# Four edits and a new instruction order in a fused decoder kernel: squared key lengths from the diagonal of the key product, weights packed on chip, row-grouped mask, padded spreading

## The chip, the cores and the metric

The kernel runs on one core of a Trainium2 chip. The metric is device time of one launch, in microseconds (us). A core has five engines that run their own instruction streams and meet only at semaphores: TensorE (PE: matrix products, with its weight loads shown as PEld), VectorE (DVE), ScalarE (ACT), GpSimd (POOL) and SyncE (SP), which here only issues DMAs.

## The reference, cut to what matters

32 sequences of 128 tokens and 256 features pass through a gated-delta-rule block with a top-2 mixture of experts (steps named `a_...` and `b_...` in the kernel), a cross attention to a context of 128 tokens, and a routed column layer (steps `c_...`). The lines that the change touches:

```python
mixed = jax.nn.silu(causal_dwconv(mixed, conv_w))          # a_conv, a_mix
q, k, v = jnp.split(mixed, [KEY_DIM, 2 * KEY_DIM], axis=-1)
q = q * jax.lax.rsqrt(jnp.sum(q * q, -1, keepdims=True) + EPS)
k = k * jax.lax.rsqrt(jnp.sum(k * k, -1, keepdims=True) + EPS)
...
# gated delta rule: S = S*exp(g); delta = (v - k S) * beta; S = S + k delta; o = q S
```

The cross attention adds a mask to its scores before the softmax over 16 heads of 16 features, and its projections use the weights Wq and Wk. The column layer picks the best of 16 columns for each token (a one-hot row) and multiplies the 1024 hidden values of the token by that row, spread from 16 to 1024 values.

## The kernel before, in words

One sequence is one item. All weights stay in SBUF. The work on an item is cut into about 75 named steps for PE and as many for the other engines; every engine runs a loop of 35 trips, and in a trip it runs the steps in the order of its list in `ORDER` (line 111). A step with `@1` works on an item one trip older than its letter says: `a` steps work on the item of this trip, `b` on the one before, `c` on the one two trips back, and the suffix gives the lag where it differs. So in a steady trip three or four items are in work, and an engine never leaves the order of its list: an instruction that waits holds up all that stands behind it. After the first trip each engine waits once, in `before_b`, for the second group of weights (semaphore `w_b`).

The steps that the change and the prediction speak of, in their order on PE:

- `a_ss`, `a_st` (lines 483 to 494): the lengths of q and k. ACT squares `mixed` into `sqk` (`a_sq`, L839, 1024 columns), PE sums it over the partitions with a 32-column block of ones (L487, four column groups of 256 columns), ACT copies the sum (L843), PE transposes it in two pieces (L493), DVE adds epsilon into `sse` (L1018). POOL's `a_sc` takes the power -0.5 of it and builds `krb`, `ckk`, `irk`, `eyec` and `pairc`.
- `a_kk` (L518): the product of the keys with themselves, four heads of 128x128 in bank A1. DVE's `a_lower` multiplies it by the decay (L1030), and `a_init` starts the triangular inverse from it (L1049 to L1060).
- `a_dec0`, `a_dec1` (L510, L511): exponents of the decay. `a_dec1` writes bank A3, in which the lengths were, and so waits for `sse_ok` first; ACT takes their exponential (L854).
- `c_wT`, `c_spread` (L748, L755): the one-hot is transposed to 16 partitions, copied by ACT (L970), and spread by eight bf16 products with a contraction of 16.
- `c_pj0`, `c_pj1` (L761): the column layer's second product; DVE's `c_gc0`, `c_gc1` (L1233) feed it. `c_weight` (L1218 to L1227) is the softmax weight, which `c_sum3` (L1239) uses.
- `b_x2T` (L623): waits for `x2`, which DVE writes in `b_x2` (L1119) behind `c_sum3`, `b_hid` (L1096) and `c_y3` (L1107 to L1103).
- `a_la..`, `a_lb..` (L535, L545): the levels of the inverse, 32x32 blocks that alternate with DVE (L1068, L1073, L1075).
- `b_dn`, then DVE's `b_ys` (L1142) and `b_y1` (L1107), `b_y1T` (L663), `b_q` (L670), with the copies of q on ACT (L919) and of k on DVE (`b_k`, L1153).
- `c_s` (L681, L685): the mask goes into four banks by four bf16 products of 512 columns with a contraction of 128 (identity times the filled mask), and the scores are added to it in four row groups of 32. Then DVE's `c_max` (L1161), ACT's `c_exp` (L926), PE's `c_pT` (L692).

At the start SP issues every load one after the other (lines 412 to 424). The weights Wq and Wk come from a DRAM layout with 16 used and 16 empty columns alternating, and 16 DMAs (`dense_qk`) gather the used ones.

## Time and profile before

| | us |
|---|---|
| median of 3 runs | 2304.79 (2304.69 to 2305.6) |
| the profiled execution | 2305.36, with a span of 2303.6 from first to last instruction |
| PE busy | 2130.6 (92%) |
| DVE busy | 1657.9 (72%) |
| ACT busy | 1374.1 (60%) |
| POOL busy | 778.8 (34%) |

The page gives for each engine the time in which it ran something. PE's figure is the largest by far, and the chain that ended last runs through PE for 77% of the span and through DVE for 14%. Busy is the time in which a matrix product was under way, and matmuls overlap in the pipeline, so two starts are closer than a duration. The page's strip of the span shows the same picture in every slice but the first two and the last ones: the kernel repeats one trip.

### The profile page before, as it was taken

How to read it: one execution, taken by the hardware profiler on the slowest of the kernel's cores; microseconds unless marked ns; L12 is line 12 of the kernel's file. 1: busy time of each engine (PE TensorE's matmuls, PEld its weight loads, DVE VectorE, ACT ScalarE, POOL GpSimd, SP SyncE). 2: the span in 40 equal slices, each digit the busy share in tenths (PEclk: the TensorE clock that was granted, in tenths of full speed). 3: DMA queues.
4: the chain of work that ended last, by engine and by line, in shares of the span. 5: the costliest groups of instructions: out<-in, count | busy, mean ns of one | idle time of the engine just before them, and what ended most of it. 6: DMA issues, size and time to landing. Idle time of an engine off the chain costs nothing.

```text
span 2303.6 us, 81126 instructions
## 1 busy us (share of the span) xinstructions
PE 2130.6 (92%) x33068; PEld 1805.7 (78%) x33130; DVE 1657.9 (72%) x5290; ACT 1374.1 (60%) x4262; POOL 778.8 (34%) x1835
## 2 busy tenths in 40 slices
PE   4799999999999999999999999999999999999976
...
DMA packets 33954, 30.12 MB, mean 13 GB/s; under 512 B 17680, under 2 KB 31008, under 8 KB 32816
## 3 DMA queue, kind: packets, MB, share of 16 engines
...
q14 instruction: 107, 0.88, 0.1%
...
## 4 chain that ended last, share of the span: by engine, by line
PE 77%; DVE 14%; ACT 4%; issue 3%; SPq 2%; POOL 1%; DVEq 0%; DMA 0%; POOLq 0%
PE bank_b L641 11%; PE bank_a L463 10%; PE bank_b L738 5%; PE bank_a L473 4%; PE bank_b L761 4%; PE bank_b L649 4%; PE bank_b L602 4%; DVE y1p L1142 3%; PE bank_a L579 3%; PE bank_a L535 3%; PE bank_a L511 3%; PE bank_b L692 3%; ACT prob L926 2%; PE bank_a L586 2%; PE bank_a L545 2%
## 5 line engine op out<-in xcount | busy, mean ns | idle before, releaser
L1013 DVE SCALAR_TENSOR_TENSOR acc<-ypad,convw,acc 128x128 f32<-128x128 f32 x1536 | 429.0, 343 | 112.4 <-ACT acc L815 112.1
L463 PE MATMUL bank_a<-xnT,wqkvz 128*128 128x128 f32 x2048 | 250.6, 279 | 2.0 <-DVE u L1089 2.0
L463 PEld LDWEIGHTS bank_a<-xnT,wqkvz 128*128 128x128 f32 x2048 | 241.4, 194 | 6.2 <-DVE u L1089 4.3
L926 ACT ACTIVATE prob<-bank_b,nmax 128x128 f32<-128x128 f32 x512 | 182.2, 381 | 39.4 <-DVE nmax L1163 38.6
L1378 POOL TENSOR_TENSOR ostat<-ostat 128x4 f32<-128x4 f32 x64 | 20.4, 320 | 504.3 <-ACT gseg L880 502.2
L1424 POOL TENSOR_SCALAR lnv<-mv 128x1 f32<-128x1 f32 x128 | 26.1, 204 | 362.5 <-DVE mv L1103 357.2
L815 ACT ACTIVATE acc<-bank_a,convw 128x128 f32<-128x128 f32 x512 | 148.0, 395 | 0.0
L535 PE MATMUL bank_a<-zblk,kkT 32*32 32x32 f32 x8192 | 119.5, 195 | 22.3 <-DVE zblk L1073 15.6
L906 ACT ACTIVATE prob<-bank_b 128x512 f32<-128x512 f32 x64 | 38.2, 597 | 167.4 <-PE bank_b L641 167.4
L535 PEld LDWEIGHTS bank_a<-zblk,kkT 32*32 32x32 f32 x8192 | 93.7, 107 | 55.8 <-issue 44.5
L545 PE MATMUL bank_a<-ablk,xblk 32*32 32x32 f32 x8192 | 120.0, 195 | 18.6 <-DMA bk<-in_bk_dram 15.1
L1161 DVE TENSOR_REDUCE smax<-bank_b 128x4 f32<-128x512 f32 x128 | 87.7, 685 | 67.8 <-PE bank_b L685 67.8
L545 PEld LDWEIGHTS bank_a<-ablk,xblk 32*32 32x32 f32 x8192 | 96.5, 107 | 49.4 <-issue 44.5
L641 PE MATMUL bank_b<-x2T,wg 128*128 128x128 f32 x1024 | 131.8, 282 | 0.0
L738 PE MATMUL bank_b<-y2T,wc 128*128 128x128 f32 x1024 | 131.2, 283 | 0.0
L641 PE MATMUL bank_b<-x2T,wu 128*128 128x128 f32 x1024 | 128.4, 279 | 0.0
L692 PE MATMUL bank_b<-const,prob 128*128 128x128 f32 x512 | 80.7, 281 | 47.2 <-ACT prob L926 47.2
L649 PE MATMUL bank_b<-wd,prob 128*128 128x256 f32 x512 | 124.1, 385 | 0.0
L738 PEld LDWEIGHTS bank_b<-y2T,wc 128*128 128x128 f32 x1024 | 123.5, 198 | 0.0
L761 PE MATMUL bank_b<-wp,prob 128*128 128x256 f32 x512 | 121.1, 380 | 1.1 <-DVE prob L1233 1.1
L1142 DVE SCALAR_TENSOR_TENSOR y1p<-bank_b,route,y1p 128x256 f32<-128x256 f32 x224 | 107.1, 478 | 20.8 <-DVE y1p L1142 0.5
L641 PEld LDWEIGHTS bank_b<-x2T,wg 128*128 128x128 f32 x1024 | 120.5, 193 | 1.3
...
## 6 DMA issues: line engine op xcount, KB each, us to landing
...
```

The lines of the kernel that those rows point to most:

```text
L463: last = mm(A[bank][:, b * P:(b + 1) * P], wqkvz[:, c, o:o + P], xnT[:, c, :], start=(c == 0), stop=(c == KC - 1))
L535: last = mm(A_LEVEL[half][r, BLK * h:BLK * (h + 1)], kkT[r, h, r], zblk[r, h, :], start=True, stop=True)
L545: last = mm(A_LEVEL[half][r, BLK * h:BLK * (h + 1)], xblk[r, h, :], ablk[r, h, :], start=True, stop=True)
L641: last = mm(Bk[bank][:, b * P:(b + 1) * P], w[:, c, o:o + P], x2T[:, c, :], start=(c == 0), stop=(c == KC - 1))
L649: mm(Bk[DOWN[e]][:, D * (b % 2):D * (b % 2) + D], act_[:, e, :], wd[:, e, :], start=True, stop=True)\
L692: last = tr(Bk[b][:, j * P:(j + 1) * P], prob[:, b, j, :], ident)
L738: last = mm(Bk[2 + half][:, b * P:(b + 1) * P], wc[:, c, o:o + P], y2T[:, c, :], start=(c == 0), stop=(c == KC - 1))
L761: last = mm(Bk[2][:, 0:D], gcw[:, b, :], wp[:, b, :], start=(b == 0), stop=(b == 7))
L815: fn(acc[:, c, :], A[bank][:, b * P:(b + 1) * P], ACT.Copy, scale=convw[:, c, TAPS - 1:TAPS])\
L926: last = fn(prob[:, j, b, :], Bk[j][:, b * P:(b + 1) * P], ACT.Exp, scale=HD ** -0.5, bias=nmax[:, 4 * j + b:4 * j + b + 1], accum_out=esu ...
L1013: stt(acc[:, c, :], ypad[:, c, k:k + P], convw[:, c, k:k + 1], acc[:, c, :], ALU.mult, ALU.add).then_inc(conv.sem, 1)
L1142: stt(y1p[:, :], Bk[DOWN[e]][:, D * (b % 2):D * (b % 2) + D], route[:, e:e + 1], y1p[:, :] if e else xh[:, :], ALU.mult, ALU.add).then_inc ...
```

## The change

1. **Key lengths from the diagonal.** `a_sq`, `a_ss`, `a_st` handle q alone: half the columns, one transpose. A new DVE step `a_kd` waits for the key product and reads the diagonal of each of the four heads with an instruction that multiplies by the identity and sums. `sse_ok` now counts five, one from `a_ss` and four from `a_kd`.
2. **Weights packed on chip.** Wq and Wk are loaded whole by two DMAs into the space of `probT`, and POOL copies the used columns in eight instructions in `before_b`.
3. **Mask in row groups.** Each bank's mask product has a contraction of 32 on its own row group.
4. **Padded spreading.** The one-hot and the spreading matrix have 128 rows, zero beyond 16; POOL clears them once.
5. **New order** of all four lists. Where the steps above stand before and after is in the lists below.

```diff
-    pe="b_v@2 b_x2T@2 a_lb01@1 a_la10@1 b_router@2 b_gu0@2 b_gu1@2 a_la11@1 a_lb10@1 b_gu2@2 a_la20@1 "
-       "a_lb11@1 b_gu3@2 b_dn0@2 a_lb20@1 a_la21@1 b_dn1@2 a_lb21@1 a_vT0@1 a_la30@1 b_k@2 a_la31@1 a_lb30@1 "
-       "a_lb31@1 b_y1T@2 a_pa@1 b_q@2 a_pb@1 c_s a_mt@1 c_pT0 a_vT1@1 a_xT a_sz0@1 c_pT1 a_ba a_qkv0 c_pT2 "
-       "a_o0@1 a_sz1@1 c_pT3 a_qkv1 a_o1@1 c_pv c_R a_z0 a_z1 c_xo a_qkv2 a_qkv3 c_y2T a_dec0 c_h a_ss c_lg "
-       "c_c0 a_st c_c1 c_wT a_kk c_spread a_dec1 c_pj0 b_oT0 b_oT1 c_pj1 b_w0 b_w1 a_la00 b_cT a_qk a_la01 "
-       "a_lb00".split(),
-    act="b_sum@2 b_cT@2 b_x2T@2 b_sg0@2 b_rl@2 b_sg1@2 b_rt@2 a_mix2@1 a_mix3@1 a_sum b_y1T@2 a_zf@1 b_q@2 "
-       "a_zo@1 c_exp0 a_mt@1 c_exp1 a_xT c_exp2 a_sz0@1 c_exp3 a_ba a_qkv0 a_o0@1 a_sz1@1 c_pT0 c_pT1 a_qkv1 "
-       "a_o1@1 c_R a_ln a_z0 a_mix0 a_z1 a_seg a_mix1 a_sq c_y2T c_h a_qkv2 a_st c_lt a_qkv3 c_c0 c_te c_wT "
-       "c_c1 a_dec0 a_dec1 b_oT0 b_oT1".split(),
-    dve="a_lb31@1 a_pa@1 b_k@2 a_u0@1 c_y4@3 c_max0 c_max1 a_xn c_max2 a_low@1 a_u1@1 c_max3 c_pT0 a_conv00 "
-       "a_conv01 c_pT1 a_conv02 c_rec a_core0@1 a_conv10 c_ao a_conv11 a_core1@1 c_sum2 a_conv12 c_y2 c_lb "
-       "c_route a_conv20 a_ss c_gc0 c_weight c_gc1 a_lower a_init c_sum3 b_hid a_la00 c_y3 b_x2 a_la01 "
-       "a_lb00 a_conv21 b_v a_conv22 a_lb01 a_conv30 a_la10 a_conv31 a_la11 a_lb10 b_act0 b_top a_conv32 "
-       "a_la20 a_lb11 a_score b_act1 b_ys0 a_la21 a_lb20 b_ys1 a_lb21 a_la30 a_la31 b_y1 a_lb30".split(),
-    pool="c_y2b@3 a_rq@1 c_ln2@3 b_xh@2 b_rs@2 b_rd@2 b_rt@2 c_ln3@3 a_xr@1 b_ln0@2 b_y1b@2 a_x a_osc0@1 a_ga "
-       "a_osc1@1 a_g c_ln1 c_rx b_mask c_sig a_sc".split(),
+    pe="a_la10@1 b_router@2 b_gu0@2 b_gu1@2 a_la11@1 a_lb10@1 b_gu2@2 a_lb11@1 a_la20@1 b_gu3@2 b_dn0@2 "
+       "a_la21@1 a_lb20@1 b_dn1@2 a_la30@1 a_lb21@1 b_k@2 a_vT0@1 a_la31@1 a_lb30@1 a_lb31@1 b_y1T@2 a_pa@1 "
+       "b_q@2 a_pb@1 c_s a_vT1@1 a_mt@1 c_pT0 a_xT a_sz0@1 c_pT1 a_sz1@1 a_ba a_qkv0 a_o0@1 a_qkv1 c_pT2 "
+       "c_pT3 a_o1@1 c_pv c_R a_z0 a_z1 c_xo a_qkv2 a_qkv3 c_y2T a_dec0 c_h c_c0 c_lg a_ss c_c1 a_st a_kk "
+       "c_wT c_spread a_dec1 c_pj0 b_oT0 b_oT1 c_pj1 b_w0 b_w1 a_la00 b_cT a_la01 a_lb00 a_qk b_v b_x2T "
+       "a_lb01".split(),
+    act="b_oT0@2 a_mix2@1 b_oT1@2 b_sum@2 b_cT@2 b_x2T@2 b_rl@2 b_sg0@2 a_sum b_sg1@2 b_rt@2 a_mix3@1 b_y1T@2 "
+       "a_zf@1 b_q@2 a_zo@1 c_exp0 a_mt@1 c_exp1 a_xT c_exp2 a_sz0@1 a_sz1@1 c_exp3 a_ba a_qkv0 c_pT0 a_o0@1 "
+       "c_pT1 a_qkv1 a_o1@1 a_ln c_R a_z0 a_mix0 a_seg a_z1 a_qkv2 c_y2T a_mix1 a_sq c_h a_qkv3 c_lt a_st "
+       "c_c0 c_c1 c_wT c_te a_dec0 a_dec1".split(),
+    dve="c_max0 a_xn c_max1 a_low@1 a_u1@1 c_max2 c_max3 a_conv00 c_pT0 c_pT1 c_rec a_conv01 a_conv02 "
+       "a_core0@1 a_conv10 c_ao a_core1@1 c_sum2 a_conv11 c_y2 a_conv12 a_conv20 a_conv21 a_conv22 c_lb "
+       "a_conv30 c_route a_ss a_kd c_gc0 c_gc1 a_lower c_weight a_init c_sum3 b_hid a_la00 c_y3 b_x2 a_la01 "
+       "a_lb00 b_v a_score b_top a_lb01 a_conv31 a_la10 a_lb10 b_act0 a_la11 a_la20 a_conv32 a_lb11 b_act1 "
+       "b_ys0 a_lb20 a_la21 b_ys1 a_lb21 a_la30 c_y4 a_la31 b_y1 a_lb30 a_lb31 a_u0 a_pa b_k".split(),
+    pool="b_xh@2 b_rs@2 a_xr@1 b_mask@2 c_ln3@3 a_rq@1 a_x b_rd@2 b_rt@2 b_ln0@2 b_y1b@2 a_ga a_osc0@1 "
+       "a_osc1@1 a_g c_ln1 c_rx c_sig a_sc c_y2b c_ln2".split(),
...
+        ssT = scoreT[:, 0, :]
...
+        raw = probT[:, :, :, :].rearrange("p a b f -> p (a b f)").rearrange("p (w k f) -> p w k f", w=2, k=KC)
+        raw_qk = [(raw[:, i, :, :], w_d) for i, w_d in enumerate((wq_d, wk_d))]
...
+            def a_kd(n):
+                dve.wait_ge(*kk_ps(n))
+                for h in range(HK):
+                    nc.vector.tensor_tensor_reduce(out=diag_junk[:, h, :], in0=A[1][:, h * P:(h + 1) * P], in1=ident, scale=1.0,
+                                                   scalar=EPS_RMS, op0=ALU.mult, op1=ALU.add, accum_out=sse[:, HK + h:HK + h + 1])\
+                        .then_inc(sse_ok.sem, 1)
...
-                mm(quad(Bk[j]), ident_bf[:, :], fill_bf[:, :].unsqueeze(1).to_broadcast([P, 4, P]), start=True, stop=False)
+                mm(quad(Bk[j]), row0_bf[r, :], fill_bf[r, :].unsqueeze(1).to_broadcast([32, 4, P]), start=True, stop=False)
...
-                tr(Bk[0][0:NCOL, 0:P], onehot[:, :], ident).then_inc(wT_ps.sem, 1)
+                tr(Bk[0][:, 0:P], onehot[:, :], ident).then_inc(wT_ps.sem, 1)
...
-            for dst, src in small_b + dense_wo + dense_qk:
+            for dst, src in small_b + dense_wo + raw_qk:
...
-                fn(sqk[:, :, :], mixed[:, 0:QK_BLOCKS, :], ACT.Square).then_inc(sq_ok.sem, 1)
+                fn(sqk[:, 0:HK, :], mixed[:, 0:HK, :], ACT.Square).then_inc(sq_ok.sem, 1)
...
-                    last = mm(A[3][32 * q:32 * q + 32, 0:2 * P], ones[:, :], sqk[:, 2 * q:2 * q + 2, :], start=True, stop=True)
+                    last = mm(A[3][32 * q:32 * q + 32, 0:P], ones[:, :], sqk[:, q, :], start=True, stop=True)
...
             def before_b():
                 pool.wait_ge(w_b.sem, W_B)
+                for i, w in enumerate((wq, wk)):
+                    for o in range(2):
+                        for c in range(2):
+                            dense = w[:, :, P * o:P * o + P].rearrange("p k (j c d) -> p k j c d", j=4, c=2)[:, :, :, c, :]
+                            padded = raw[:, i, :, P * (2 * o + c):P * (2 * o + c) + P].rearrange("p k (j t) -> p k j t", j=4)[:, :, :, 0:HD]
+                            ts(dense, padded, 1.0, 0.0, ALU.mult, ALU.add).then_inc(packed.sem, 1)
```

## Rows read from the trace of the kernel before

**Rows 1.** The page, busy time: us (share of the span) x instructions.
```profile
PE 2130.6 (92%) x33068; PEld 1805.7 (78%) x33130; DVE 1657.9 (72%) x5290; ACT 1374.1 (60%) x4262; POOL 778.8 (34%) x1835
```
**Rows 2.** Busy time by stretch (a clock drop, one steady trip); PEclk is the granted share.
```profile
753.10:756.50 3.40, 3.40 (x27) 1.67 (x21) 0.00 (x0) 2.04 (x3) 0.00 (x0) 0.50 0.14 43
...
1000.00:1067.85 67.85, 64.98 (x1034) 55.48 (x1035) 51.62 (x166) 42.78 (x133) 24.20 (x57) 1.00 0.03 8
```
**Rows 3.** Waits of PE over the span: total us, times, longest.
```profile
PE bank_b L692 <- ACT prob L926: 47.2, 36, 2.5
```
**Rows 4.** Timeline of PE, lengths to `c_pj0`: start us, us, engine line, operation.
```profile
1056.56 0.64 PE L487 MATMUL bank_a<-scoreT,ones 128*32 128x256 f32 x8
1057.12 0.40 PE L744 MATMUL bank_b<-w,hT 128*128 128x16 f32 x2
...
1059.24 0.38 PE L493 MATMUL bank_a<-const,scoreT 128*128 128x128 f32 x2
...
1061.35 1.06 PE L518 MATMUL bank_a<-mixed 128*128 128x128 f32 x8
1062.34 0.62 PE L755 MATMUL bank_b<-wT,spread_bf 16*128 16x128 bf16 x8
1063.12 1.02 PE L511 MATMUL bank_a<-gseg,const 128*128 128x512 f32 x2 [0.16 <-issue]
1063.97 1.89 PE L761 MATMUL bank_b<-wp,prob 128*128 128x256 f32 x8
```
**Rows 5.** Timeline of ACT in the same stretch.
```profile
1064.13 1.09 ACT L854 ACTIVATE decay<-bank_a 128x512 f32<-128x512 f32 x2
```
**Rows 6.** Timeline of DVE from `c_weight` to `c_sum3`.
```profile
1063.38 0.17 DVE L1218 TENSOR_SCALAR lg<-lg 128x16 f32<-128x16 f32 x1
...
1063.94 0.18 DVE L1223 CUSTOM_DVE_ANT_0 lg<-lg,lrec 128x16 f32<-128x16 f32 x1
1064.04 0.08 DVE L1223 DVE_READ_ACCUMULATOR2_ANT lsm<- 128x1 f32 x1
1064.16 0.16 DVE L1227 RECIPROCAL lsm<-lsm 128x1 f32<-128x1 f32 x1
1064.24 0.69 DVE L1233 TENSOR_TENSOR prob<-prob,bank_b 128x512 f32<-128x512 f32 x1
1065.32 1.23 DVE L1030 TENSOR_TENSOR kkT<-bank_a,decay 128x1024 f32<-128x1024 f32 x1 [0.39 <-ACT decay L854]
...
1070.34 0.44 DVE L1239 SCALAR_TENSOR_TENSOR y3p<-bank_b,lsm,y2pb 128x256 f32<-128x256 f32 x1
```
**Rows 7.** Timeline of PE at `b_x2T`.
```profile
1075.57 0.44 PE L623 MATMUL bank_b<-const,x 128*128 128x128 f32 x2 [0.26 <-DVE x L1119]
```
**Rows 8.** Timeline of PE, mask and scores.
```profile
1030.05 1.04 PE L681 MATMUL bank_b<-fill_bf,ident_bf 128*128 128x512 bf16 x4
1031.02 1.15 PE L685 MATMUL bank_b<-kT,qT 32*128 32x256 f32 x16
```
**Rows 9.** Timeline of ACT, copy of q ahead of the scores.
```profile
1029.53 0.63 ACT L919 ACTIVATE qT<-bank_b,bq 128x128 f32<-128x128 f32 x2
```
**Rows 10.** Timeline of DVE around the scores.
```profile
1028.78 1.12 DVE L1153 SCALAR_TENSOR_TENSOR kT<-bank_b,bk,madj 128x128 f32<-128x128 f32 x4
...
1030.41 0.41 DVE L1107 TENSOR_SCALAR yout<-y,mv,lnv 128x256 f32<-128x256 f32 x1
```
**Rows 11.** Timeline of SP's queue at the start: start us, us, DMAs issued.
```profile
34.07 5.26 SPq L422 DMA_DIRECT2D wq<-in_wq_dram  x8
39.37 4.36 SPq L422 DMA_DIRECT2D wk<-in_wk_dram  x8
```
**Rows 12.** Timeline of PE at the start, the wait for the second weights.
```profile
60.14 0.65 PE L545 MATMUL bank_a<-ablk,xblk 32*32 32x32 f32 x32 [15.07 <-DMA bk<-in_bk_dram]
```
**Rows 13.** Timeline of POOL, `a_sc` from its first to its last instruction.
```profile
1061.95 1.71 POOL L1307 TENSOR_TENSOR rqk<-sse,nhalf 128x8 f32<-128x8 f32 x1 [2.71 <-DVE sse L1018]
...
1064.97 0.62 POOL L1352 TENSOR_TENSOR pairc<-const,ckk 128x256 f32<-128x256 f32 x1
```

More of the change, by code:

```diff
@@ L306, in build @@
         w_a, w_b = sig("weights_a"), sig("weights_b")
+        packed = sig("packed", 8)
         wqkvz_in = [sig(f"wqkvz_in{g}") for g in range(6)]
@@ L323, in build @@
         ssT_ok, st_ps = sig("ssT_ok"), sig("st_ps")
-        sq_ok, ss_ps, sse_ok, rqk_ok, kscale = sig("sq_ok"), sig("ss_ps"), sig("sse_ok"), sig("rqk_ok"), sig("kscale", 5)
+        sq_ok, ss_ps, sse_ok, rqk_ok, kscale = sig("sq_ok"), sig("ss_ps"), sig("sse_ok", 1 + HK), sig("rqk_ok"), sig("kscale", 5)
         vT_ps, u_ok = sig("vT_ps", 2), sig("u_ok", 2)
@@ L363, in build @@
                     for j in range(4) for c in range(2)]
-        dense_qk = [(w[:, :, P * o:P * o + P].rearrange("p k (j c d) -> p k j c d", j=4, c=2)[:, i, :, c, :],
-                     w_d.rearrange("p k (a j t) -> p k a j t", a=4, j=4, t=32)[:, i, 2 * o + c, :, 0:HD])
-                    for w, w_d in ((wq, wq_d), (wk, wk_d)) for i in range(KC) for o in range(2) for c in range(2)]
+        raw = probT[:, :, :, :].rearrange("p a b f -> p (a b f)").rearrange("p (w k f) -> p w k f", w=2, k=KC)
+        raw_qk = [(raw[:, i, :, :], w_d) for i, w_d in enumerate((wq_d, wk_d))]
         dense_b = [(b[32 * j + HD * c:32 * j + HD * c + HD, o:o + 1], b_d[32 * j:32 * j + HD, 2 * o + c:2 * o + c + 1])
@@ L491, in a_st @@
                 pe.wait_ge(*ssT_ok(n))
-                for e in range(2):
-                    last = tr(A[3][:, (2 + e) * P:(3 + e) * P], ssT[:, e, :], ident)
-                last.then_inc(st_ps.sem, 1)
+                tr(A[3][:, 2 * P:3 * P], ssT, ident).then_inc(st_ps.sem, 1)
             def values(n, half):
@@ L653, in b_k @@
                 pe.wait_ge(*ysum(n, 2))
+                if first(n):
+                    pe.wait_ge(*packed(1))
                 for b in range(2):
@@ L667, in b_q @@
                 pe.wait_ge(*y1T_ok(n))
+                if first(n):
+                    pe.wait_ge(*packed(1))
                 for b in range(2):
@@ L969, in c_wT @@
                 act.wait_ge(*wT_ps(n))
-                fn(wT[:, :], Bk[0][0:NCOL, 0:P], ACT.Copy).then_inc(wT_ok.sem, 1)
+                fn(wT[:, :], Bk[0][:, 0:P], ACT.Copy).then_inc(wT_ok.sem, 1)
             def before_b():
@@ L1017, in a_ss @@
                 dve.wait_ge(*st_ps(n))
-                ts(sse[:, :].rearrange("p (q e) -> p q e", e=2),
-                   A[3][:, 2 * P:4 * P].rearrange("p (e q r) -> p q e r", q=4, r=32)[:, :, :, 0], EPS_RMS, None, ALU.add).then_inc(sse_ok.sem, 1)
+                ts(sse[:, 0:HK], A[3][:, 2 * P:3 * P].rearrange("p (q r) -> p q r", r=32)[:, :, 0], EPS_RMS, None, ALU.add)\
+                    .then_inc(sse_ok.sem, 1)
[4 more added lines that the diff above has]
+                                                   scalar=EPS_RMS, op0=ALU.mult, op1=ALU.add, accum_out=sse[:, HK + h:HK + h + 1])\
+                        .then_inc(sse_ok.sem, 1)
             def values(n, half):
@@ L1278, in before_b @@
                 ts(wout[:, :, :], wout[:, :, :], gnw[:, 0:1], None, ALU.mult).then_inc(wout_ok.sem, 1)
-            steps = dict(a_xn=a_xn, a_ss=a_ss, a_lower=a_lower, a_score=a_score, a_init=a_init, a_pa=a_pa, a_low=a_low, b_hid=b_hid, c_rec=c_rec, b_v=b_v,
+            steps = dict(a_xn=a_xn, a_ss=a_ss, a_kd=a_kd, a_lower=a_lower, a_score=a_score, a_init=a_init, a_pa=a_pa, a_low=a_low, b_hid=b_hid, c_rec=c_rec, b_v=b_v,
                          b_x2=b_x2, b_top=b_top, b_k=b_k, b_y1=b_y1, c_ao=c_ao, c_sum2=c_sum2,
```

28 lines of the change are left out of this document (17 added, 11 removed).

## The prediction

> **What bounds the kernel now.** I read the busy times first: PE is at work for 92% of the span, DVE for 72% [rows 1]. Then one steady trip: of 67.85 us PE is busy for 64.98, at the full clock of 2.4 GHz (granted share 1.00) [rows 2]. So PE's list sets the trip, and there are only 2.9 us a trip in which it does nothing. The waits say where: 47.2 us over the span, about 1.5 a trip, ahead of the first transposes of the probabilities (L692), where the chain scores, `c_max`, `c_exp` is late [rows 3]; and 0.26 at `b_x2T`, which waits for DVE's `x2` [rows 7]. The others are tenths. Two things follow. PE work that goes is time gained only if PE does not wait for it elsewhere. And a wait that is added anywhere on PE's list is lost in full, since there is no slack that takes it up. DVE has slack on the average but not at `b_x2T`: there it is DVE's chain `a_lower`, `a_init`, `c_sum3`, `c_y3`, `b_x2` that ends last.
>
> The profiled execution took 2305.36 us for a span of 2303.6, 0.6 above the median; I add to it and take 0.6 off.
>
> **The mask (part 3).** The four products start at 1030.05 and the scores at 1031.02, so 0.97 us [rows 8]. The scores themselves are four row groups at a time: 16 records of 256 columns in about 1.1 us, where a 128-row product would take them one after the other [rows 8]. So I take it that the four masks stream together: one product's 0.24 (a quarter of 0.97), and a little for the switch. But they can't all start: bank 3 waits for `q_ok`, and the copy of q ends at 1030.16 [rows 9]; the copy of k ends at 1029.90 [rows 10]. The fourth mask then starts at about 1030.2 and the scores at 1030.45: 0.57 us gained. If row groups did not overlap here, 0.
>
> **The tail ahead of it (part 5).** `c_y4` (0.41 us, L1107) stood behind `b_k` and `a_u0`, where DVE then idles until the scores [rows 10]. Now it stands between `a_la30` and `a_la31`, ahead of `b_y1`, from which y1T, q and the scores follow. DVE is packed there; I charge 0.2, half of it, since `a_la31` also had to wait for PE; bounds 0 and 0.41. `a_u0` goes between `a_lb31` and `a_pa`, into a gap. Together with the mask: 0.57 - 0.20 = 0.37 gained a trip.
>
> **From the scores to `c_xo` (part 5).** `a_vT1` goes ahead of `a_mt` into the 1.5 us wait. But the next thing, `c_pT1`, waits for ACT's second group of exponentials, whose start is tied to the scores and not to PE, and the steps of PE before it are the same set as before. So the wait moves and does not shrink. Later, ACT copies `c_pT0` ahead of `a_o0`, and DVE does two convolution steps ahead of `a_core0`, so `c_ao` comes no earlier. I take 0; a third of the 1.5 us either way (0.5) are the bounds.
>
> **Lengths (part 1), what goes.** PE's sums took from 1056.56 to 1057.12, 0.56 us; with half the columns about 0.33, so 0.23 less. One transpose of two goes: 0.11 (half of 1059.24 to 1059.45) [rows 4]. ACT loses half of a square and of a copy, which lie beside PE's column products. 0.33 of PE time gained, up to the end of `c_c1`.
>
> **Lengths, what comes.** This decides the prediction. Before, after `c_c1` PE ran at once: `c_wT` 1061.24, `a_kk` 1061.35, `c_spread` 1062.34, `a_dec1` (first record kept 1063.12), `c_pj0` 1063.97 [rows 4]. From the end of `a_kk` (1062.24: eight records 0.11 apart from 1061.35) to `c_pj0` that is 1.73 us. Now the order is `a_st`, `a_kk`, `c_wT`, `c_spread`, `a_dec1`, and `a_dec1` waits for all five of `sse_ok`, so for `a_kd`, which waits for `a_kk`. All that PE has between them is 0.11 for `c_wT` and 0.45 for `c_spread`, and behind the waiting `a_dec1` stand `c_pj0`, `b_oT`, `b_w` and the rest of the trip.
> What does `a_kd` take? The trace has this instruction in a small form: the multiply and sum over 16 elements starts at 1063.94, its accumulator read at 1064.04, the next instruction at 1064.16: 0.22 us [rows 6]. Four of those are 0.88, the lower bound. A two-input instruction of 128 elements from PSUM starts every 0.26 us (four in 1.12, less the last one's tail of 0.08) [rows 10]; with a read of 0.12 behind each, four take 1.5, and with nothing overlapped (0.34 + 0.12) 1.85, the upper bound. I take 1.4, near the row of 128 elements. With 0.25 for PE's last result to reach DVE and for the way back, `a_dec1` starts 1.65 after the end of `a_kk`, where PE had 0.56 to do. It takes 1.09 itself (its weights to `c_pj0`, 0.22 + 0.85). So `c_pj0` comes 2.74 after `a_kk` in place of 1.73; `a_st` now stands ahead of it and `c_wT` behind, which is even. PE: +1.0, less the 0.33 above: `c_pj0` 0.7 later than in a trip before. The lower bound gives +0.2.
>
> The Trainium skill prices the body of such an instruction (VectorE: DVE Perf Modes, the section on the TRN2 errata) at 120 cycles plus one per element at 0.96 GHz for a source in PSUM, 0.26 us for 128 elements. The row of 128 elements shows the same 0.26, so this case's trace agrees; by the page's 58 cycles for a source in SBUF it would be 0.19, and the whole step 0.3 us shorter.
>
> **DVE behind it.** `a_lower` started at 1065.32, released by ACT's second exponential [rows 5, 6], so it comes 0.2 later with `a_dec1` (ACT's pair was late before, too: it started at 1064.13, after a table load). Then `c_weight`, 0.86 us (1063.38 to 1064.24), which stood between `c_gc0` and `c_gc1`, where DVE had room, now stands between `a_lower` and `a_init` [rows 6]. So `a_init` and `c_sum3` come 1.06 later. POOL's `a_sc` takes 3.64 us from its first to its last instruction [rows 13] and starts some 1.4 later than `sse_ok` did; it ends before `a_init` needs it. What is late next is `b_x2T`: PE gets there 0.7 later, DVE's `x2` 1.06 later, and PE already waited 0.26 for it [rows 7]. So +1.06 from there to the mask. This holds in part even with a short `a_kd`: `c_weight` alone moves `x2` by 0.8.
>
> **Spreading (part 4).** With 128 rows the array is not switched to 16 rows and back. Before, there is a gap of 0.10 ahead of L755 and 0.16 behind it [rows 4]. Both lie now inside the wait for `a_kd`: nothing.
> The Trainium skill says (TensorEngine Tiling (Array Packing), Key Properties) that changing the tiling mode drains TensorE. The two gaps agree with it; by that rule the padding would be worth 0.26 us a trip if nothing waited there, 8 us in all.
>
> **Start (part 2).** PE stands from 45.07 to 60.14 for the second weights, 15.07 us [rows 12], and the loads are bound by SP's issuing: sixteen DMAs for Wq and Wk take 5.26 + 4.36 = 9.62 us of its time [rows 11]. Two take their place, 0.66 each by the dearer row (5.26 / 8), 1.3 in all: 8.3 gained, since only the bias loads stand behind. They move four times the bytes in use; if the transfers were the bound, nothing would be gained, so 0 to 9.6. POOL's eight packing instructions have half the elements of L1352 (0.62) [rows 13], 2.5 to 5 us, needed a trip later. With the convolutions that now run before that wait and not behind it, I take 10 in all.
>
> **Sum.** A trip: +1.06 - 0.37 = +0.69. Times 31 steady trips: +21. Start: -10. So 2305.4 + 11 = 2316, and against the median 2315.5.
>
> **The rivals.**
> - *PE's savings count in full* (faster). If `a_kd` is at its lower bound, and `x2` is not the last at `b_x2T`, a trip loses 0.57 + 0.33 + 0.26 of PE work and keeps 0.2 for `c_y4`: -0.96, -30 in all, -40 with the start: 2265. For it: PE is the bound on the page [rows 1]. Against it: the two orders of steps above. Partly true, with 0.4 a trip gained or 0.3 lost, it gives 2283 to 2304. Chance of faster 0.26.
> - *The two halves cancel.* With `a_kd` at 0.88, a trip loses 0.8 - 0.37 = 0.4, +13, which the start takes back: 2308; with half a tenth more gained around the exponentials, 2305. Within 0.2%: 0.17.
> - *The clock* (slower still). In some trips the granted share falls to 0.50 (1.2 GHz) for 3.4 us, where PE did light work with waits: at 753.10 it had 27 matmul records in 3.4 us [rows 2]. Each such stretch costs about 1.7 us. The new waits around `c_spread`, two of about 0.5 us, make a second thin place in the trip. If every second trip falls there, 16 x 1.7 = +27: 2342. In place of that, masks that do not overlap: +0.57 x 31 = +18, 2334. Together 0.14.
> - *The forecast*, 0.43.
>
> Slower has 0.57, within 0.2% (4.6 us, about what a measurement of this kernel can tell from no change) 0.17, faster 0.26. The range leaves out the outer half of the faster case and of the clock case: 2278 to 2340.
>
> **What would show it.** Right: in a steady trip of the changed kernel PE idles ahead of `c_spread` and of `a_dec1`, the latter released by DVE; `a_kd`'s eight records take 1.3 to 1.5 us; the wait at `b_x2T` grows from 0.26 to 0.6; the mask stretch falls to about 0.4 us; the second weights arrive near 52 us; a trip is 68.5 us. Wrong: `a_dec1` follows `c_spread` without a gap, or `b_x2T` waits no longer than before. What would sink the sum is a `c_xo` that comes 0.5 earlier than I took it, since no row shows that stretch in its new order.

## The result and the profile after

The changed kernel takes 2323.7 us, median of nine runs (2314.3 to 2333.5), against 2306.6 for the kernel before in nine (2298.9 to 2309.8): a ratio of 1.0076, 95% interval 1.0052 to 1.0099. It is slower by 17 us. The forecast was 2315.5, in the range 2278 to 2340, with slower as the likeliest sign.

The page of the changed kernel, busy times, granted clock by slices and the shares of the chain that ended last:

```profile
PE 2139.0 (92%) x33036; PEld 1805.3 (78%) x33098; DVE 1698.2 (73%) x5547; ACT 1373.2 (59%) x4262; POOL 798.8 (34%) x1845
...
PEclk8799999999999999999999999999999999999987
...
PE 58%; DVE 24%; ACT 11%; issue 5%; POOL 2%; DVEq 0%; POOLq 0%; ACTq 0%
```

Its span is 2325.3 us, 21.7 above the one before. PE is as busy as it was [rows 1], but the chain that ended last now runs through DVE for 24% of the span, 14% before. The waits of PE (total us, times, longest) say where, beside the wait ahead of the probabilities' transposes (L698, 47.2 before [rows 3]):

```profile
PE bank_b L624 <- DVE x L1132: 28.8, 31, 0.9
PE bank_b L698 <- ACT prob L932: 24.6, 37, 2.3
PE bank_a L536 <- DVE zblk L1086: 24.3, 33, 1.7
PE bank_b L761 <- ACT wT L976: 12.3, 32, 0.6
```

L624 is `b_x2T`: PE waits there 0.9 us in every trip, where it waited 0.26 [rows 7]. L761 is `c_spread`, which now waits 0.37 us in every trip for ACT's copy of the one-hot; before, that wait was 0.7 us over the whole span. One trip without a clock drop, busy time by engine, answers to [rows 2]:

```profile
964.19:1032.52 68.33, 64.85 (x1036) 55.02 (x1039) 52.82 (x173) 42.72 (x134) 24.77 (x57) 1.00 0.03 8
```

It is 68.33 us long, the shortest trip of this kernel; before, the shortest was 67.67. The same trip in PE's timeline, from the key product to `c_pj0`, at `b_x2T`, and from the masks to the scores (these answer to [rows 4], [rows 7] and [rows 8]):

```profile
994.32 1.06 PE L519 MATMUL bank_a<-mixed 128*128 128x128 f32 x8
995.21 0.27 PE L754 MATMUL bank_b<-const,onehot 128*128 128x128 f32 x1
995.86 0.62 PE L761 MATMUL bank_b<-wT,spread_bf 128*128 128x128 bf16 x8 [0.37 <-ACT wT L976]
996.63 1.02 PE L512 MATMUL bank_a<-gseg,const 128*128 128x512 f32 x2 [0.16 <-issue]
997.49 1.03 PE L767 MATMUL bank_b<-wp,prob 128*128 128x256 f32 x4
...
1009.99 0.44 PE L624 MATMUL bank_b<-const,x 128*128 128x128 f32 x2 [0.94 <-DVE x L1132]
...
1032.30 0.55 PE L687 MATMUL bank_b<-fill_bf,row_bf 32*128 32x512 bf16 x4
1032.52 1.73 PE L691 MATMUL bank_b<-kT,qT 32*128 32x256 f32 x16
```

The masks now take 0.22 us to the first score product, 0.97 before: the four row groups run together. `c_spread` is preceded by a wait for ACT. Ahead of `a_dec1` no wait for DVE is shown, but its first product (L511) is missing from this trace in all but 2 of 64 cases; what hides there, 0.10 us, comes out further down. DVE in the same trip, with the new `a_kd` (L1030) and `c_weight` (L1231 to L1240) between `a_lower` (L1043) and `a_init` (L1062):

```profile
995.41 0.29 DVE L1030 CUSTOM_DVE_ANT_0 diag_junk<-bank_a,const 128x128 f32<-128x128 f32 x1 [0.34 <-PE bank_a L519]
995.63 0.08 DVE L1030 DVE_READ_ACCUMULATOR2_ANT sse<- 128x1 f32 x1
995.63 0.29 DVE L1030 CUSTOM_DVE_ANT_0 diag_junk<-bank_a,const 128x128 f32<-128x128 f32 x1
...
996.26 0.08 DVE L1030 DVE_READ_ACCUMULATOR2_ANT sse<- 128x1 f32 x1
996.29 1.28 DVE L1246 TENSOR_TENSOR prob<-prob,bank_b 128x512 f32<-128x512 f32 x2
998.50 1.22 DVE L1043 TENSOR_TENSOR kkT<-bank_a,decay 128x1024 f32<-128x1024 f32 x1 [0.92 <-ACT decay L860]
999.64 0.41 DVE L1231 TENSOR_SCALAR lg<-lg 128x16 f32<-128x16 f32 x1
...
1000.45 0.29 DVE L1236 CUSTOM_DVE_ANT_0 lg<-lg,lrec 128x16 f32<-128x16 f32 x1
...
1000.79 0.16 DVE L1240 RECIPROCAL lsm<-lsm 128x1 f32<-128x1 f32 x1
1000.87 2.10 DVE L1062 TENSOR_TENSOR diag<-kkT,ckk 32x256 f32<-32x256 f32 x4
```

Two readings. `a_kd` takes 0.93 us from 995.41 to 996.34, not 1.4: the four stand 0.21 apart, and each accumulator read lies beside the next one. And `c_weight` takes 1.23 us (999.64 to 1000.87) where the same instructions took 0.86 [rows 6]: its first one has 0.41 instead of 0.17, and the multiply and sum 0.29 instead of 0.18. POOL at that time:

```profile
999.40 0.62 POOL L1366 TENSOR_TENSOR pairc<-const,ckk 128x256 f32<-128x256 f32 x1
999.98 0.73 POOL L1458 TENSOR_TENSOR y2pb<-y,rows 128x256 f32<-128x256 f32 x1
1000.67 0.72 POOL L1458 TENSOR_TENSOR y2lb<-y,rows 128x256 f32<-128x256 f32 x1
```

These are the last instruction of `a_sc` and the two of `c_y2b`. The first instruction of `c_weight` runs beside the former, its multiply and sum and the first product of `a_init` beside the latter. The experiments come back to them.

For what follows I use offsets: the start of a step behind the first score product of its trip, median over the trips that are at most 0.25 us longer than the shortest of their kernel. They are starts in the timelines, subtracted.

| us | before | changed |
|---|---|---|
| second transposes `c_y2T` | 23.27 | 23.58 |
| logits product of `c_lg` | 26.02 | 27.55 |
| key product | 30.24 | 30.13 |
| `c_spread` | 31.23 | 31.67 |
| `c_pj0` | 32.87 | 33.30 |
| `a_lower` (DVE) | 34.21 | 34.31 |
| `a_init` (DVE) | 35.47 | 36.68 |
| `b_x2T` | 44.47 | 45.81 |
| mask | 66.71 | 68.19 |
| shortest, mean trip | 67.67, 68.61 | 68.33, 69.56 |

### The profile page after: what moved, and what is told of

Read it like the earlier page. It is cut to its first block, busy times and chain, and to the rows that moved or that the text cites. A ratio compares the mean times of both kernels' runs of the same rounds, so it can differ in the third digit from the quotient of the medians.

```text
span 2325.3 us, 81316 instructions
## 1 busy us (share of the span) xinstructions
PE 2139.0 (92%) x33036; PEld 1805.3 (78%) x33098; DVE 1698.2 (73%) x5547; ACT 1373.2 (59%) x4262; POOL 798.8 (34%) x1845
## 4 chain that ended last, share of the span: by engine, by line
PE 58%; DVE 24%; ACT 11%; issue 5%; POOL 2%; DVEq 0%; POOLq 0%; ACTq 0%
PE bank_b L642 11%; PE bank_a L466 10%; PE bank_b L744 5%; DVE y1p L1155 5%; PE bank_a L476 4%; ACT prob L932 4%; DVE diag L1062 3%; PE bank_a L587 2%; PE bank_b L698 2%; PE bank_b L675 2%; DVE bn L1114 2%; PE bank_a L536 2%; PE bank_a L546 2%; ACT L860 2%; PE bank_b L723 2%
## 5 line engine op out<-in xcount | busy, mean ns | idle before, releaser
L1019 DVE SCALAR_TENSOR_TENSOR acc<-ypad,convw,acc 128x128 f32<-128x128 f32 x1536 | 422.9, 346 | 157.1 <-ACT acc L821 155.7
L920 ACT ACTIVATE y1T<-bank_b 128x256 f32<-128x256 f32 x32 | 12.3, 385 | 290.6 <-PE bank_b L666 290.6
L1338 POOL TENSOR_TENSOR gate<-ba,dtb 128x8 f32<-128x8 f32 x32 | 6.6, 206 | 426.8 <-ACT ba L832 426.8
L767 PE MATMUL bank_b<-wp,prob 128*128 128x256 f32 x512 | 121.1, 380 | 1.1 <-DVE prob L1246 1.1
L642 PEld LDWEIGHTS bank_b<-x2T,wu 128*128 128x128 f32 x1024 | 120.1, 193 | 1.3
```

The lines of the kernel that those rows point to most:

```text
L642: last = mm(Bk[bank][:, b * P:(b + 1) * P], w[:, c, o:o + P], x2T[:, c, :], start=(c == 0), stop=(c == KC - 1))
L767: last = mm(Bk[2][:, 0:D], gcw[:, b, :], wp[:, b, :], start=(b == 0), stop=(b == 7))
L1019: stt(acc[:, c, :], ypad[:, c, k:k + P], convw[:, c, k:k + 1], acc[:, c, :], ALU.mult, ALU.add).then_inc(conv.sem, 1)
```

## The experiments

The theory to test was the prediction's: `a_dec1` waits for `a_kd`, and `c_weight` in front of `a_init` delays `x2`; against it, that the order does the damage by itself, or that the clock does. Each comparison is with the kernel before on the same chip, whose medians were 2306.2 to 2307.3.

### The parts one at a time

Part 3 alone.

```diff
-mm(quad(Bk[j]), ident_bf[:, :], fill_bf[:, :].unsqueeze(1).to_broadcast([P, 4, P]), start=True, stop=False)
+mm(quad(Bk[j]), row0_bf[r, :], fill_bf[r, :].unsqueeze(1).to_broadcast([32, 4, P]), start=True, stop=False)
```

The mask is the same in all rows of an item, and `row0_bf` is one in the first row of each group of 32 and zero elsewhere, so a contraction of 32 hands that row to all 128.

> The kernel before with the row-grouped mask alone (part 3). Prediction's term: the scores start 0.57 us earlier in a trip, because the fourth mask waits for the copy of q; trip 67.77 to 67.2 us, 31 trips: -18, about 2288 us. The trace of the changed kernel shows 0.23 us from the first mask to the scores in place of 0.97: if the copy of q does not hold it up here either, -0.74 a trip, 2283 us. Rival, masks do not overlap: no change, 2306. Rival, clock: the tail of the trip gets thinner and the granted clock falls to 0.50 in more trips than before (before: 8 places in the steady trips, 9 stretches of 3.4 us); then the clean trips are 0.6 to 0.7 shorter, but the total is only 5 to 10 us below before.

Measured: 2286.7 us (ratio 0.991, 0.990 to 0.993), between the two totals expected. The shortest trip falls from 67.67 to 66.85, the scores start 0.23 behind the masks. The gain arrives in full in a trip without a clock drop, 0.8 us; over 31 trips that would be 25 us, and 20 are measured. The trace holds 18 stretches of 3.4 us at half clock in the steady trips, 9 before, which is where the clock rival would look for the rest.

Part 2 alone.

```diff
-for dst, src in small_b + dense_wo + dense_qk:
+for dst, src in small_b + dense_wo + raw_qk:
```

> The kernel before with part 2 alone: Wq and Wk loaded whole by two DMAs and packed by GpSimd. Forecast by the prediction's term: TensorE's wait for the second weights falls from 15.07 us to 6.8 (8.3 less), the trips unchanged (67.67 the shortest), the total 8 us below before, 2296 to 2301. By the pair mask_alone and parts234 (9.7 us apart, with a wait of 14.3 and of 6.9): 7 to 10 us below. Rival (the four times larger transfers bound it, or GpSimd's packing holds up its list): 2304 to 2308.

Measured: 2298.9 us (ratio 0.9975, 0.9962 to 0.9987), 7.3 below. SP's queue and PE's wait at the start:

```profile
34.39 0.58 SPq L422 DMA_DIRECT2D probT<-in_wq_dram  x1
35.02 0.44 SPq L422 DMA_DIRECT2D probT<-in_wk_dram  x1
...
52.23 0.65 PE L545 MATMUL bank_a<-ablk,xblk 32*32 32x32 f32 x32 [4.23 <-DMA bk<-in_bk_dram]
```

Two issues of 1.0 us in place of 9.6 [rows 11]; the second weights are there at 52.2, as forecast, instead of 60.14 [rows 12]. PE's wait is 4.23 us and not 6.8, since PE got there 2.9 us later. The transfers were not the bound. They move twice the bytes and not four times: two of 512 KB in place of sixteen of 32 KB.

The new order of the four lists alone, without `a_kd`.

```diff
-dve="... c_lb c_route a_conv20 a_ss c_gc0 c_weight c_gc1 a_lower a_init c_sum3 ...
+dve="... a_conv30 c_route a_ss c_gc0 c_gc1 a_lower c_weight a_init c_sum3 ...
```

> The kernel before with all four new lists, without a_kd and the four edits. If the new order itself is what costs (c_weight between a_lower and a_init, DVE's chain last at b_x2T): b_x2T waits about 0.9 us, a clean trip is 67.77 + 1.3 = 69.1 us, the total 2340 to 2350. If a_kd's wait ahead of a_dec1 is what costs, as the larger term of the prediction has it: a trip of 67.8 to 68.1, the total 2305 to 2315.

Measured: 2360.0 us (ratio 1.022, 1.0199 to 1.0241), 10 above the expected range. The shortest trip is the expected one, 69.13 us; the mean trip is 1.54 above it, 0.94 before. The order alone costs 53 us, and the edits take most of it back.

### The four corners

Parts 2, 3 and 4 without the new way of the lengths, in the old order; all four edits in the old order; and parts 2, 3 and 4 in the new order. The fourth corner is the changed kernel.

```diff
-dve="... c_route a_conv20 a_ss c_gc0 c_weight ...
+dve="... c_route a_conv20 a_ss a_kd c_gc0 c_weight ...
```

> The packed weights, the row-grouped mask and the padded spreading in the old order, without the lengths from the diagonal. With the mask alone a run took 2286.7 us. If the padding gives back the gaps around c_spread (0.10 and 0.16 us) where nothing else waits there, and the packed weights 8 us at the start: 2286.7 - 8 - 8 = about 2271 us, a clean trip 66.6 us. If the padding is worth nothing (the gaps are another wait, such as ACT's copy of the one-hot): 2279 us and 66.85.

> All four edits in the old order, with a_kd behind a_ss on DVE. If the lengths from the diagonal cost by themselves (PE has only c_spread, about 0.5 us, between a_kk and a_dec1, and a_kd takes 0.93 and the ways there and back 0.25): a_dec1 0.7 later, less 0.33 of PE work, so 0.4 to 1.0 us a trip more than the same kernel without them, 2283 to 2300 us. If the order alone is what costs, this is as fast as or faster than the kernel without the lengths, 2260 to 2271 us.

> The new order of all four lists with parts 2, 3 and 4 (weights packed on chip, row-grouped mask, padding), and the lengths as in the kernel before (no a_kd, squares and sums of q and k). It completes four corners: old order without and with the lengths from the diagonal 2277.1 and 2303.3 us, new order with them 2323.7, and this one. Theory (the lengths cost in the old order since a_dec1 waits for them and a_init waits for a_sc; in the new order c_wT, c_spread and ACT's copy stand between a_kk and a_dec1, so that there the new way of the lengths costs nothing, and what it spares on TensorE, 0.65 us of the key product's start as between the kernel order_alone and the changed kernel, counts until b_x2T): the first product behind the decay at 33.8 us of the trip, x2 at 45.6 to 45.9, bound by c_weight in front of a_init as in the changed kernel, the clean trip 68.2 to 68.6 us, the total 2318 to 2332. Rival (the costs of the lengths and of the order simply add): 2323.7 - 26 = 2297, clean trip 67.4.

| median us (ratio to before, interval) | lengths as before | lengths from the diagonal |
|---|---|---|
| old order | 2277.1 (0.986, 0.983 to 0.989) | 2303.3 (0.998, 0.996 to 1.001) |
| new order | 2324.7 (1.008, 1.005 to 1.011) | 2323.7 (1.008, 1.005 to 1.010) |

The first is near the 2279 expected for a padding that is worth nothing. The second is 3 above its range; its shortest trip is 0.88 longer than without the diagonal, 0.4 to 1.0 expected. The third is inside the range of its theory, and 28 above what adding the costs gives.

The costs do not add. In the old order the diagonal costs 26 us, in the new one nothing; the order costs 48 us with the old lengths and 20 with the new. The offsets tell how:

| us | old order, parts 2 to 4 | old, all edits | new, parts 2 to 4 | changed |
|---|---|---|---|---|
| `c_ao` on DVE | 16.68 | 16.68 | 18.39 | 18.40 |
| `c_y2T` | 23.26 | 23.26 | 23.56 | 23.58 |
| `c_lg` | 26.01 | 25.80 | 27.71 | 27.55 |
| key product | 30.24 | 29.92 | 30.71 | 30.13 |
| `c_pj0` | 32.66 | 33.09 | 33.77 | 33.30 |
| `a_init` | 35.51 | 35.73 | 37.05 | 36.68 |
| `b_x2T` | 44.41 | 45.36 | 45.78 | 45.81 |

*Old order, diagonal.* The key product comes 0.32 earlier, as the prediction counted (0.33), but then PE stands. All four edits in the old order, PE's timeline and the total of that wait:

```profile
988.42 0.61 PE L761 MATMUL bank_b<-wT,spread_bf 128*128 128x128 bf16 x8
989.61 0.39 PE L511 MATMUL bank_a<-below_bf,ident_bf 128*128 128x512 bf16 x1 [0.58 <-DVE sse L1030]
...
PE bank_a L511 <- DVE sse L1030: 19.5, 32, 1.0
```

This is the wait for `a_kd` of the forecast, 0.6 us a trip, in the order for which the prediction had not counted it.

*New order.* The key product now stands ahead of `c_wT`, so ACT's copy of the one-hot is no longer covered by it. Parts 2 to 4 in the new order, PE:

```profile
992.21 0.27 PE L755 MATMUL bank_b<-const,onehot 128*128 128x128 f32 x1
992.85 0.62 PE L762 MATMUL bank_b<-wT,spread_bf 128*128 128x128 bf16 x8 [0.37 <-ACT wT L977]
```

PE pays 0.37 with or without `a_kd`. This wait, `c_wT` and `c_spread` stand between the key product and `a_dec1`, and `a_kd` is all but done in that time: 0.93 us of DVE's time, begun 0.20 behind the point at which PE goes on from the key product to `c_wT` (995.21). Further ahead, DVE's `c_ao` comes 1.7 us later, since `a_conv01` and `a_conv02`, which stood around `c_pT1` ahead of `c_rec`, now stand behind `c_rec`. PE stands 0.17 in `c_xo` for it (1.04 us to the next step, 0.86 before), and `c_y2T` comes 0.3 later. And `c_lg` behind `c_c0` puts the logits 1.7 later, and `c_wT` 1.5. The key product is 0.47 later; 0.3 of it is `c_y2T`'s, the rest I did not trace.

### The two steps of the prediction

`a_dec1` of the changed kernel waits for `a_ss` alone.

```diff
-pe.wait_ge(*sse_ok(n))
+pe.wait_ge(*sse_ok(n, 1))
```

> The changed kernel in which a_dec1 waits for the one read of its bank that a_ss makes and no longer for a_kd. By the prediction's term (PE waits for a_kd's 1.4 us ahead of a_dec1): a_dec1 0.5 to 1.0 us earlier. By the trace of the changed kernel, where a_kd takes 0.93 us and a_dec1's product starts 0.776 after c_spread's, as it did before (0.774): no wait there, no change, 2324 us and a trip of 68.3. DVE's chain would hide a gain at b_x2T in either case, so the place to look at is the start of c_pj0 in the trip, +33.30 us from the scores: 33.3 or 32.5.

Measured: 2321.3 us (ratio 1.006, 1.0038 to 1.0081), 2.3 below the changed kernel and inside its spread. `c_pj0` comes 0.12 earlier, `b_x2T` 0.03. From the last spreading product to `a_dec1`'s second product it is 0.27 us, 0.37 in the changed kernel: the wait for `a_kd` was there and took 0.10. The wait that was to decide the prediction is worth next to nothing here.

`c_weight` back between `c_gc0` and `c_gc1`.

```diff
-a_ss a_kd c_gc0 c_gc1 a_lower c_weight a_init
+a_ss a_kd c_gc0 c_weight c_gc1 a_lower a_init
```

> The changed kernel with c_weight moved back between c_gc0 and c_gc1 on DVE, nothing else. Theory (DVE's chain is last at b_x2T because of c_weight): a_init and x2 come 1.1 to 1.2 us earlier, PE reaches b_x2T at +44.94 us of the trip and waits no longer, trip 68.33 - 0.86 = 67.5, total about 2297, faster than both. Rival (PE's wait at c_spread and a_dec1 sets the trip alone): no change, 2324. Rival (c_gc1 0.9 later holds up b_oT0 and c_pj1 on PE): between, 2310 or more.

Measured: 2310.7 us (ratio 1.002, 0.9997 to 1.0046). 13 us come back, about half of what 0.8 a trip would give, against about 2297 by the theory, and `b_x2T` moves only from 45.81 to 45.55. The number is the third outcome's (`c_gc1` holds up PE), the reason is not: the next experiment leaves `c_gc1` where it is here, and `b_x2T` comes 0.8 earlier. DVE at `a_init` of this kernel, and POOL beside it:

```profile
991.86 1.23 DVE L1043 TENSOR_TENSOR kkT<-bank_a,decay 128x1024 f32<-128x1024 f32 x1
993.48 2.59 DVE L1062 TENSOR_TENSOR diag<-kkT,ckk 32x256 f32<-32x256 f32 x4 [0.40 <-POOL pairc L1366]
...
992.76 0.62 POOL L1366 TENSOR_TENSOR pairc<-const,ckk 128x256 f32<-128x256 f32 x1
993.34 0.72 POOL L1458 TENSOR_TENSOR y2pb<-y,rows 128x256 f32<-128x256 f32 x1
994.03 0.90 POOL L1458 TENSOR_TENSOR y2lb<-y,rows 128x256 f32<-128x256 f32 x1
```

Two things took the place of `c_weight`. `a_init` waits 0.40 for `a_sc`, which starts only when `a_kd` has delivered the lengths. And the four products of `a_init` take 2.59 us where they take 1.71 alone; the first two run beside `c_y2b` and take 0.86 and 0.85 each.

### What runs beside the chain

The suspicion was that POOL's `c_y2b` slows DVE. In the changed kernel, and in the one with `c_weight` back, it goes right behind `c_rx`, ahead of `c_sig` and `a_sc`.

```diff
-a_osc1@1 a_g c_ln1 c_rx c_sig a_sc c_y2b c_ln2
+a_osc1@1 a_g c_ln1 c_rx c_y2b c_sig a_sc c_ln2
```

> The changed kernel with POOL's c_y2b ahead of c_sig and a_sc, where POOL idles, and nothing else. Theory: c_y2b's two additions (0.73 us each) run beside DVE's c_weight and a_init and slow them: the first instruction of c_weight takes 0.41 us in place of 0.17 and the first of a_init 0.80 in place of 0.41. Then those come down, x2 comes 0.6 us earlier, b_x2T's wait falls from 0.86 to 0.25, trip 67.7, total about 2304 us. Rival (the durations have another cause, ACT's or the first use of a tile): no change in them, 2324 us.

> The same with c_weight moved back as well. In the kernel with c_weight back alone (2310.7 us), DVE waited at a_init for POOL's a_sc until +35.9 us of the trip, and the first two instructions of a_init took 0.86 us each beside c_y2b. Theory: with c_y2b out of the way they take 0.41, x2 comes 0.9 us earlier than there, and b_x2T is bound by PE: +44.9, trip 67.45, total about 2297 us. Rival (the wait for a_sc is the rest): 2305 us or more.

Measured: 2309.4 us (ratio 1.000, 0.998 to 1.002) and 2298.3 us (0.995, 0.992 to 0.998). Moving two instructions of POOL gives 14 us in the changed kernel, as much as moving `c_weight`; both together give 25. `b_x2T` comes at 45.28 and 44.78. The first product of `a_init` falls from 0.80 to 0.41 us and the multiply and sum of `c_weight` from 0.29 to 0.17, as expected. The first instruction of `c_weight` does not: it keeps its 0.41, since it ran beside `pairc` of `a_sc` and not beside `c_y2b`. With `c_weight` back, the groups of `a_init`'s products without and with the move, one edit apart (line and form: busy us, mean ns, idle before and its releaser):

```profile
L1062 DVE TENSOR_TENSOR diag<-kkT,ckk 32x256 f32<-32x256 f32 x128 | 79.8, 624 | 13.4 <-POOL pairc L1366 12.0
```
```profile
L1062 DVE TENSOR_TENSOR diag<-kkT,ckk 32x256 f32<-32x256 f32 x128 | 53.3, 417 | 13.6 <-POOL pairc L1366 12.2
```

The same move in the two kernels of the old order, in the second one with the wait of `a_dec1` reduced as above:

```diff
-pool="c_y2b@3 a_rq@1 ... c_ln1 c_rx b_mask c_sig a_sc"
+pool="a_rq@1 ... c_ln1 c_rx c_y2b b_mask c_sig a_sc"
```

> The kernel parts234 (all of the change but the lengths from the diagonal, in the order of before; 2277.1 us) with one more move: c_y2b, the copies of the second residual for a_x2, stands right behind the last copy of rx on GpSimd's list instead of in the tail. In parts234 the first product of x2 in a trip comes 44.41 us behind the trip's first score product and TensorE waits some 0.45 us for VectorE there, 14.1 us in all. Theory (VectorE's chain through a_weight and a_init is lengthened by GpSimd's copies running beside it): TensorE's wait there falls to under 5 us in all, x2 comes at about 44.0, the clean trip falls from 66.83 to about 66.4 us, the total to 2262 to 2270. Rival (the copies cost the same wherever they stand, and the chain is bound by the scores' table load): 2274 to 2280 with the same wait. A third outcome: the copies now hold up the weights of a_sc or a pair product earlier in the trip; then the start of a_init moves later than in parts234 and the total is above 2280.

> The kernel all_old (all four edits in the order of before; 2303.3 us against 2277.1 without the lengths from the diagonal) with two of the suspected costs of the lengths taken away: the first step of the decay waits only for a_ss instead of for a_kd as well, and c_y2b stands right behind the last copy of rx. Theory (the lengths cost by who waits for them and by what runs beside the chain, not by their own time on VectorE): the first product behind the decay comes at 32.3 to 32.7 us of the trip (33.1 in all_old, 32.66 without the lengths), x2 at 44.2 to 44.6 (parts234 44.41), the clean trip 66.6 to 67.0, the total 2265 to 2282. Rival (the 0.93 us of VectorE's time that a_kd takes ahead of its part of the decay are the cost, whoever waits): that product stays within 0.15 us of 33.1 and the total stays at or above 2290. In between: GpSimd's a_sc still begins late because it waits for the lengths, so a_init waits for it: x2 near 45, total 2282 to 2290.

Measured: 2265.7 us (2260.2 to 2269.2; ratio 0.9815, 0.9788 to 0.9841), the fastest kernel of the study, and 2282.8 us (0.990, 0.987 to 0.992), at the edge between the two outcomes written down. In the first, the total is in the range of its theory, but the parts are smaller: PE's wait at `b_x2T` falls from 14.1 to 8.3 us in all and not under 5, the shortest trip to 66.63 and not 66.4. The products of `a_init` over the whole span, first all edits in the old order, then the same with the move and the reduced wait, then parts 2 to 4 with the move:

```profile
L1062 DVE TENSOR_TENSOR diag<-kkT,ckk 32x256 f32<-32x256 f32 x128 | 79.4, 620 | 17.5 <-POOL pairc L1366 16.1
```
```profile
L1062 DVE TENSOR_TENSOR diag<-kkT,ckk 32x256 f32<-32x256 f32 x128 | 54.1, 423 | 20.9 <-POOL pairc L1366 19.7
```
```profile
L1056 DVE TENSOR_TENSOR diag<-kkT,ckk 32x256 f32<-32x256 f32 x128 | 53.3, 417 | 2.4
```

From a mean of 620 ns to 423: (620 - 423) x 4 = 0.79 us a trip on the chain to `x2`. Two edits lie between these two kernels, but the pair above shows the same fall by the move alone. In parts 2 to 4 the mean was 458 without the move, because there `c_y2b` comes earlier and lies beside the first product only. The wait for `pairc`, 19.7 us, stays: it is the diagonal's own price on POOL's side. The wait of `a_dec1` is gone, but not the time behind it. This is what released `c_pj0` (L767) in the second of the three kernels, over the span (PE's weight loads counted with it):

```profile
L767 PE MATMUL bank_b<-wp,prob x512: 379/379/483, 168.6 to 2268.8; 128*128 128x256 f32 x171
...
  DVE prob L1246: 30.6, 34
```

The next to be late is `c_gc0`, which stands behind `a_kd` on DVE: `c_pj0` starts 1.40 us behind the last spreading product, 1.13 in parts 2 to 4 with the move. That eats the key product's lead, and no more: `c_pj0` comes at 32.54, inside the 32.3 to 32.7 expected and level with the 32.59 of parts 2 to 4 with the move; 33.09 was the rival's. What is left is at `a_init`, which waits for `pairc`: it starts at 35.68 against 35.45, and `b_x2T` at 44.43 against 44.17. So the diagonal costs 17 us more than the old way even then. With 66.85 against 66.63 for the shortest trips, 7 of them are in the trips' own length; the means, 67.90 and 67.51, give 12. The rest I did not trace. Between the second kernel and the changed one with both moves, 2298.3, lie 15 us more: that much stays of the new order, and no run isolates which of its other moves cost it.

One trip of the fastest kernel, as [rows 2]:

```profile
1215.44:1282.30 66.86, 64.27 (x1039) 55.31 (x1038) 51.29 (x166) 42.90 (x134) 23.92 (x57) 1.00 0.03 8
```

## Why the prediction was right, and where it was not

**Right in sign and in the size of a trip.** Forecast +0.69 us a trip; the shortest trips are 0.66 apart. Where it was to be seen was mostly right too: the wait at `b_x2T` (0.94, 0.6 forecast), `a_lower` unmoved (+0.1, held by ACT's table load; 0.2 forecast), the weights at the start, the mask.

That the trip agrees to 0.03 us is luck. `b_x2T` comes 0.28 later than forecast, the stretch behind it gains 0.23 more than forecast, and the two misses cancel. The number for `a_dec1` in the sum, 0.2 at `a_lower`, was small enough that its wrong working did no harm.

**The mask and `c_y4`.** 0.74 instead of 0.57. The fourth mask product does wait for the copy of q and starts 0.16 behind the first, but the scores start 0.06 behind it and do not wait until it has run through. For `c_y4` I charged 0.2: from `b_x2T` to the mask it is 22.24 us before and 22.38 after, so all that the new order does in that stretch costs 0.14 together; no run takes `c_y4` alone. Together with the mask 0.6 gained, 0.37 forecast.

**The wait of `a_dec1` failed.** The step was "`a_dec1` starts 1.65 after the end of `a_kk`, where PE had 0.56 to do". Two terms were wrong. `a_kd` was taken at 1.4 us, near the row of 128 elements from PSUM; it takes 0.93, near the lower bound, because each accumulator read runs beside the next instruction. The 0.25 for the ways there and back was about right: 0.20 from the key product to `a_kd` and under 0.1 back. And I called the swap of `a_st` and `c_wT` even. It exposes ACT's copy of the one-hot, 0.37 us, in which all but 0.10 of the wait for `a_kd` then hides. The text named idle time ahead of `c_spread` as a sign but put no price on it. So `c_pj0` came 0.43 later and not 0.7, and for another reason: taking the wait away gives 0.12.

The Trainium skill's price for the body (VectorE: DVE Perf Modes, the section on the TRN2 errata), 0.26 us for 128 elements from PSUM, does not hold for this instruction: the four start 0.21 us apart, the reads included. Its 0.19 for a source in SBUF is the nearer one.

**`c_weight` was right as far as it went.** It delays `a_init`, by 1.2 us against `a_lower` moved by 0.1. I took 0.86; it takes 1.23, with 0.25 more from the start of its first instruction to the next and 0.12 more in its multiply and sum, both beside POOL. The sentence "it ends before `a_init` needs it", on `a_sc`, held only because `c_weight` was in the way: with it back, `a_init` waits for `pairc` 29 times. `b_x2T` +1.34, forecast +1.06.

**What was missing is what POOL runs beside the chain.** `c_y2b` did not move against `a_sc`: it stood first in the old list, so directly behind the `a_sc` that ends the list, and stands directly behind it now. But the diagonal delivers the lengths later, and POOL's steps slide with them: `a_sc` starts 32.24 us behind the scores, 30.84 before, and `c_y2b` 35.79, 34.45 before. There it meets `c_weight` and `a_init`: the first product of `a_init` takes 0.80 us, 0.66 before, and `c_weight` the 0.37 above, 0.25 of it beside `a_sc`. The prediction had the later start of `a_sc` right (1.4) and asked only whether `a_sc` ends in time, not what it and `c_y2b` do to DVE. In the new order this is what the diagonal's gain turned into: with it `c_pj0` comes 0.47 earlier than without, `a_init` 0.37 earlier, and its products take 2.10 us instead of 1.70, so `b_x2T` is where it was (45.81 and 45.78).

**From the scores to `c_xo`, taken as 0 within 0.5.** `c_xo` starts 0.04 later, although PE's wait ahead of the probabilities' transposes halves (24.6 us, 47.2 before): nothing came of that. `c_y2T` is 0.3 later, inside the bounds; 0.17 of it is PE's stand in `c_xo`, because `c_ao` is 1.7 later on DVE. "`c_ao` comes no earlier" was read only on its good side.

**The padding** was put at nothing, because both gaps would lie in a wait. Without such a wait nothing arrives either. Between the kernel with the mask alone and the one with parts 2 to 4, the step from the last key product to the spreading shrinks from 0.21 to 0.11 us, and from the last spreading product to `a_dec1`'s second one from 0.37 to 0.27. `c_pj0` comes 0.14 earlier and `b_x2T`, where DVE is last, 0.01 later. The gap of 0.16 behind the spreading [rows 4] was misread: `a_dec1`'s first product runs in it (L510), of which that trace keeps 2 of 64 records; where all 64 are kept, in parts 2 to 4, it follows the spreading by 0.06 without a gap. The Trainium skill's drain at a change of tiling mode (TensorEngine Tiling (Array Packing), Key Properties) agrees with 0.10 at each of the two changes, 0.20 a trip and not 0.26.

**The start** gave 8.7 us (first scores at 131.8 instead of 140.5), 10 forecast. The prediction's "four times the bytes" is twice, as above; the forecast did not rest on it.

**The rest is the clock.** The nine times of the changed kernel go from 2314.3 to 2333.5 with the mean granted clock of each run, 0.974 to 0.964. In its profile the steady trips hold 18 stretches of 3.4 us at half clock, 9 before. The mean trip is 1.23 above the shortest, 0.94 before: 0.29 x 31 = 9 us, about what the forecast is short of. Busy time in one such stretch:

```profile
1239.70:1246.50 6.80, 6.80 (x93) 5.34 (x87) 2.80 (x9) 4.14 (x9) 0.00 (x0) 0.50 0.02 4
```

The clock rival had the sign right and the place wrong. It expected new drops around `c_spread`; all twelve places lie at the end of a trip and the start of the next, from 66.3 us on, where PE has the tail of the inverse and then waits for the exponentials. What makes them more frequent I did not isolate: the kernel with the mask alone has 13 such places with 18 stretches, the one with parts 2 to 4 has 8 with 10, and both are faster than before.

**The rival that PE's savings count in full** put the time at 2265. A kernel of that time exists, 2265.7, but it has the old order and the old lengths, so it is not that rival come true.
